# Routed expert layer in two halves of tiles, with the neighbouring stages' work between its slots

## What is computed

```python
x = x + tanh(g_xattn[2]) * L2_xattn(layernorm(x), ctx, ctx, ...)      # L2: 16 heads, one shared key/value head
x = x + tanh(g_ffn[2])   * L2_ffn(layernorm(x), switch_w, ..., w1, b1, w2, b2)   # F2: the routed experts
x = x + tanh(g_xattn[3]) * L3_xattn(layernorm(x), ctx, mask, ...)     # L3: causal, with masked queries
x = x + tanh(g_ffn[3])   * L3_ffn(layernorm(x), ...)                  # F3: butterfly weights

# L2_ffn: of 8 experts each token uses the one with the largest probability
logits = t @ switch_w + switch_b
route_prob = softmax(logits)
y_e = gelu(t @ w1[e] + b1[e]) @ w2[e] + b2[e]
out = y_(argmax e) * max(route_prob)
```

## Time and profile before

| | us |
|---|---|
| runs, median (lowest to highest) | 1117.06 (1116.2 to 1119.53) |
| profiled execution, first to last instruction | 1124.8 |
| TensorE / VectorE / ScalarE / POOL busy | 932.1 / 754.2 / 677.1 / 454.1 |
| end of L2's statistics to L3's first scores | 691.5 to 844.3 |

### The profile page before, as it was taken

One profiled execution on the slowest core, in us unless ns is written; L12 is line 12 of the kernel. 1 busy time (PEld: TensorE's weight loads), 2 busy tenths in 40 slices (PEclk: granted clock), 3 DMA queues, 4 the chain that ended last, 5 costly groups with the idle time before them and its releaser, 6 DMA issues.

```text
span 1124.8 us, 29016 instructions
## 1 busy us (share of the span) xinstructions
PE 932.1 (83%) x9406; PEld 555.3 (49%) x9416; DVE 754.2 (67%) x2004; ACT 677.1 (60%) x1462; POOL 454.1 (40%) x975
## 2 busy tenths in 40 slices
PE   3898889885758565799999886599958999999899
PEld 3644444443436333344545443277733555454698
DVE  3566777756978799778887772355584666667444
ACT  3556666646856566767776641155535777775466
POOL 5411112241134434301244344344458988877300
PEclk9999999995559777899999995599989999999999
DMA  6977656429999300000000000112131111111011
GB/s 186 155 88 82 47 45 47 38 29 238 179 181 174 97 1 1 1 1 2 2 15 15 14 11 19 39 51 60 54 84 58 40 58 40 59 55 43 6 36 35
DMA packets 285283, 67.07 MB, mean 60 GB/s; under 512 B 206241, under 2 KB 277985, under 8 KB 285154
## 3 DMA queue, kind: packets, MB, share of 16 engines
q1 hardware_dynamic: 279394, 50.94, 29.6%
q0 software_dynamic: 4896, 14.18, 3.7%
q10 hardware_dynamic: 864, 0.27, 0.1%
HBM read 34.80 MB, written 30.56 MB: 58 GB/s over the span
## 4 chain that ended last, share of the span: by engine, by line
PE 57%; DVE 21%; issue 8%; POOL 6%; ACT 3%; DMA 2%; SPq 2%; another core or an unknown queue 1%; DVEq 0%; ACTq 0%; POOLq 0%
PE bank L1132 14%; DVE nmax L1580 8%; PE bank L1164 6%; PE bank L1446 3%; PE bank L1431 3%; PE bank L1248 3%; PE bank L1146 3%; PE bank L1486 3%; PE bank L1478 2%; DVE stats L1515 2%; DVE small L1760 2%; PE bank L1257 2%; PE bank L1135 2%; PE bank L1122 2%; PE bank L1439 2%
## 5 line engine op out<-in xcount | busy, mean ns | idle before, releaser
L1580 DVE TENSOR_REDUCE nmax<-bank 128x8 f32<-128x1024 f32 x192 | 234.8, 1223 | 129.1 <-PE bank L1135 126.4
L823 ACT ACTIVATE probs_space<-bank 128x1024 f32<-128x1024 f32 x192 | 196.7, 1024 | 153.5 <-PE bank L1146 152.6
L1132 PE MATMUL bank<-q_one,k_all 32*128 32x512 f32 x768 | 221.5, 646 | 30.3 <-DVE nmax L1580 27.4
L1135 PE MATMUL bank<-k_one,q_all 32*128 32x512 f32 x768 | 218.4, 643 | 2.4 <-DVE nmax L1580 1.1
L1164 PEld LDWEIGHTS bank<-probs_space,vals 128*32 128x32 f32 x3072 | 74.3, 110 | 125.7 <-issue 124.1
L1164 PE MATMUL bank<-probs_space,vals 128*32 128x128 f32 x3072 | 127.8, 284 | 0.0
L1132 PEld LDWEIGHTS bank<-q_one,k_all 32*128 32x128 f32 x768 | 62.6, 187 | 59.9 <-issue 57.9
L833 ACT ACTIVATE k_one<-k_all,one_head 128x512 f32<-128x512 f32 x96 | 68.8, 722 | 20.8 <-DVE k_all L1606 19.3
L1146 PE MATMUL bank<-nmax_one,ones_bf 12*128 12x512 bf16 x384 | 79.3, 385 | 0.0
L576 POOL TENSOR_TENSOR var_b<-stats 128x8 f32<-128x8 f32 (+3 forms) x32 | 7.2, 225 | 178.4 <-DVE stats L1515 176.2
L649 POOL CAST nmax_parts<-nmax 128x16 bf16<-128x16 f32 x64 | 12.7, 199 | 162.9 <-DVE nmax L1580 121.4
(11 more groups left out here) (282 smaller groups left out, 2248.7 us busy)
## 6 DMA issues: line engine op xcount, KB each, us to landing
expert_rows<-zeros SPq DMA_DIRECT2D x8, 2128.5 KB, 31.8
late<-in_L_ffn_up_weights_dram POOLq DMA_DIRECT2D x9, 512.0 KB, 4.1
late<-_L_ffn_down_weights_dram POOLq DMA_DIRECT2D x9, 512.0 KB, 4.2
q_one<-expert_rows SPq DMA_DIRECT2D x40, 64.5 KB
q_scratch<-late SPq DMA_DIRECT2D x8, 256.0 KB
v_scratch<-moe_w SPq DMA_DIRECT2D x8, 256.0 KB, 3.4
vals<-v_scratch SPq DMA_DIRECT2D x8, 256.0 KB, 6.9
o_scratch<-o_tok SPq DMA_DIRECT2D x32, 64.0 KB, 3.1
```

Source lines behind the costliest of these rows:

```text
L823: act.activation(probs[:, 2 * g:2 * g + 2, :, :].rearrange("k g i q -> k (g i q)"), bank_pair[1][:, :, :].rearrange("k g f -> k (g f)"), A ...
L1132: pe.matmul(bank[2 + s], group(k_all, u, 2 * g + s), group(q_one, u, 2 * g + s), start=not masked, stop=False)
L1135: m = pe.matmul(bank[s], group(q_all, v, 2 * f + s), group(k_one, v, 2 * f + s), start=not masked, stop=True)
L1580: dve.tensor_reduce(nmax[:, u % 2, 0, :].rearrange("q (g i) -> q g i", i=HG)[:, 2 * g:2 * g + 2, :], bank_pair[0][:, :, :].rearrange("q g ...
```

## The change

- **Two halves.** PARTS = 2: tiles 0 to 15 and 16 to 31 have their own regions in expert_rows, their own slot table and 23 slots each, NS = 46. starts_0 and ends hold the row sums per half.
- **Routing between slots.** L2 is run up to iteration 33; iterations 34 to 40 stand before slot steps -2, 5, 6, 7, 8, 9 and 11 (ROUTE_BEFORE) on TensorE, ScalarE and VectorE. POOL does the rows and scatters of the last two quads after its slots 3, 5, 7 and 9. The slots start on the first half's table alone. VectorE makes the second table in four blocks at steps 12 to 15.
- **Expert weights stationary.** VectorE copies the slot's expert's w1 (128x512) within SBUF to hid2, with a register load of its own (of_next); TensorE multiplies its four 128-column parts, stationary, with the transposed slot, so the result is already transposed. The four transposes (L1439) and the copy out of PSUM (L1883) go, the seven fill products too. VectorE now has two register loads per slot.
- **Masks** of L3 in six blocks at steps 16 to 21; keep_rep lies in three other buffers. W_con is loaded before L1 rather than at the end of L2, and transposed at step 13.
- **Return.** The first half's rows are loaded by SP before slot 31 and added by VectorE two tiles at a time at steps 30 to 37; POOL makes norms of the first 16 tiles after its slots 31, 33 and 37. The second half's rows are added inside L3, at its iterations 2 to 8; their norms are made by POOL at its tiles 7 and 12.
- **Head of L3.** Iterations -10 to -7 run before step 36, -6 to -3 before steps 40 to 43 (LAST_HEAD), on TensorE and ScalarE; the fill products of the head go.
- **POOL's schedule in L3**: three butterfly steps a tile only up to step 18, then four; none at tiles 7, 12 and 18, which have a norm.

```diff
...
+        ROUTE_BEFORE = {-2: NT + 2, 5: NT + 3, 6: NT + 4, 7: NT + 5, 8: NT + 6, 9: NT + 7, 11: NT + 8}
+        SECOND_TABLE_FROM, TRANSPOSED_AT, MASKS_FROM = 12, 13, 16
+        RETURN_FROM = 30
+        LAST_HEAD = {NS - 10: range(-X_LEAD, -6), NS - 6: (-6,), NS - 5: (-5,), NS - 4: (-4,), NS - 3: (-3,)}
...
@@ SP
                 for s_no in range(NS):
+                    if s_no % NS_PART == 0:
+                        part = s_no // NS_PART
+                        sp.wait_ge(S("R_slots"), part + 1)
+                        for c in range(4):
+                            sp.wait_ge(S(f"scattered_{c}"), 16 * QT * (part + 1))
+                    if s_no == NS_PART + RING:
+                        returned_rows(0)
...
@@ POOL, beside_last_attention
-                pool.wait_ge(S("B_res"), NT)
+                pool.wait_ge(S("R_gate"), PARTS)
...
-                    if v == 16:
+                    if v == 7:
+                        norms(6 * NT, 16, 24, keep_scale=True)
+                    elif v == 12:
+                        norms(6 * NT, 24, NT, keep_scale=True)
+                    elif v == 18:
                         norms(7 * NT, 0, 8)
-                    for _ in range(3 if k < 6 * STAGES else 4):
+                    for _ in range(0 if v in (7, 12, 18) else 3 if k < 2 * STAGES else 4):
...
@@ POOL, after the indirect DMA of slot s_no
+                    if s_no == 3:
+                        rows_of_quad(NQ - 2)
+                    elif s_no == 5:
+                        scatter(NQ - 2)
+                    elif s_no == 7:
+                        rows_of_quad(NQ - 1)
+                    elif s_no == 9:
+                        scatter(NQ - 1)
+                    elif s_no == 11:
+                        pool.wait_ge(S("t_pv"), 2 * 2 * NT)
+                        pool.iota(column_no, [[-HR, HG], [1, P]], base=0, channel_multiplier=0,
...
@@ ScalarE
-                for t in range(-2, iterations("L2").stop):
+                for t in range(-2, NT + 2):
...
                 for t in range(-2, NS):
+                    if t in ROUTE_BEFORE:
+                        iteration(ROUTE_BEFORE[t])
+                    for i in LAST_HEAD.get(t, ()):
+                        last_iteration(i)
...
+                routing_weights(1)
...
@@ TensorE
-                load_expert(0)
-                fill_wait(7)
+                pe.wait_ge(S("t_mx"), 2 * 2 * NT)
+                pe.wait_ge(S("t_ex"), 2 * 2 * NT)
                 for t in range(-2, NS + 1):
...
+                    if t == TRANSPOSED_AT:
+                        last_weights()
...
                     if live(t + 1, NS):
                         pe.wait_ge(S("G_xe"), t + 2)
-                        past(pe, "G_hs", t)
-                        pe.matmul(bank[(t + 1) % 2][:, :], xnT[:, (t + 1) % 2, :],
-                                  moe_w1[:, bass.ds(expert[t + 1] * HID, HID)], start=True, stop=True
-                                  ).then_inc(S("G_hp"), 1)
...
+                        past(pe, "G_ge", t)
+                        pe.wait_ge(S("G_w1"), t + 2)
                         for c in range(NC):
...
+                            m = pe.matmul(bank[(t + 1) % 2][:, c * P:(c + 1) * P],
+                                          hid2[:, (t + 1) % 2, c * P:(c + 1) * P], slot_xT[:, (t + 1) % 2, :],
+                                          start=True, stop=True)
+                        m.then_inc(S("G_hp"), 1)
+                    load_expert(t)
...
@@ VectorE
+                for t in range(-2, NS + 1):
+                    if t in ROUTE_BEFORE:
+                        iteration(ROUTE_BEFORE[t])
+                    if live(t + 2, NS):
+                        if t + 2 == NS_PART:
+                            dve.wait_ge(S("R_slots"), 2)
+                        of_next = dve.value_load(expert_int[0:1, t + 2:t + 3], min_val=0, max_val=NE - 1)
+                        past(dve, "G_hp", t + 1)
+                        dve.tensor_copy(hid2[:, t % 2, :], moe_w1[:, bass.ds(of_next * HID, HID)]).then_inc(S("G_w1"), 1)
                     if live(t + 1, NS):
-                        dve.wait_ge(S("G_hp"), t + 2)
-                        past(dve, "G_ht", t)
-                        dve.tensor_copy(hid[:, (t + 1) % 2, :], bank[(t + 1) % 2][:, :]).then_inc(S("G_hs"), 1)
+                        dve.wait_ge(S("G_xt"), t + 2)
...
+                    if 0 <= t - SECOND_TABLE_FROM < 4:
+                        slot_table(1, t - SECOND_TABLE_FROM)
+                    if 0 <= t - MASKS_FROM < 6:
+                        last_masks(t - MASKS_FROM)
+                    if 0 <= t - RETURN_FROM < NT_PART // 2:
+                        add_returned(2 * (t - RETURN_FROM), 2 * (t - RETURN_FROM) + 2)
...
+                iteration = attention("L3")
+                for t in range(-2, iterations("L3").stop):
+                    if t == -2:
+                        gates_of(1)
+                    if 2 <= t < 5:
+                        add_returned(NT_PART + 3 * (t - 2), NT_PART + min(3 * (t - 1), GC))
+                    if 5 <= t < 9:
+                        add_returned(NT_PART + GC + 2 * (t - 5), NT_PART + GC + 2 * (t - 4))
+                    iteration(t)
```

More of the change, by code:

```diff
@@ L817, in quad_bank @@
                 def quad_bank(c):
-                    return bank[2] if own and c == 0 else bank[5]
+                    return bank[2] if layer == "L2" and c == 0 else bank[5]
                 def exponentials(u, g):
@@ L911, in attention @@
                 return iteration
-            def run(layer):
-                iteration = attention(layer)
-                for t in iterations(layer):
-                    iteration(t)
             def bit_ffn(layer, gated, steps, next_iteration=None):
@@ L1392, in _ @@
             if "L2" in phases:
[L1393 removed]
+                for t in range(-2, NT + 2):
                     iteration(t)
             if "F2" in phases:
[L1396 to L1401 removed]
+                last_iteration = attention("L3")
                 pe.wait_ge(S("t_ve"), NQ)
@@ L1450, in _ @@
             if "L3" in phases:
-                run("L3")
+                for t in range(-2, iterations("L3").stop):
+                    last_iteration(t)
             if "F3" in phases:
@@ L1592, in by_group, with iteration @@
                     return ap.rearrange("q (g i) -> q g i", i=HG)
-                for t in iterations(layer):
-                    if between is not None and t > NT:
-                        between(t - 1)
+                def iteration(t):
                     u, v, w = t - lag, t + 2, t - R_XT
@@ L1694, in attention @@
                             dve.sem_inc(S("wsum"), 1)
+                return iteration
             def mask_rows():
@@ L1800, in first_steps @@
                     bit_ffn("F0", False, range(t - NT - 4, t - NT - 3))
-            attention("L0", first_steps)
+            iteration = attention("L0")
+            for t in iterations("L0"):
+                if t > NT:
+                    first_steps(t - 1)
+                iteration(t)
             if "F0" in phases:
@@ L1839, in _ @@
             if "L2" in phases:
-                attention("L2")
+                iteration = attention("L2")
+                for t in range(iterations("L2").start, NT + 2):
+                    iteration(t)
             if "F2" in phases:
-                dve.wait_ge(S("R_start"), NQ)
-                link(dve.tensor_scalar(fill[:, 0, :], starts[:, QT, :], 1.0 / P, (P - 1) / P - 0.498, ALU.mult, ALU.add))
-                link(dve.tensor_scalar(fill[:, 0, :], fill[:, 0, :], MAGIC, None, ALU.add))
@@ new lines, in add_returned @@
+                def add_returned(first, last):
+                    part = first // NT_PART
+                    for t in range(first, last):
+                        at = (t - part * NT_PART) * P
+                        if t % GC == 0:
+                            dve.wait_ge(S(f"chunk_in{t // GC}"), 32)
+                        dve.scalar_tensor_tensor(out=x[:, t * P:(t + 1) * P], in0=returned[part][:, at:at + P],
+                                                 scalar=gate[:, t:t + 1], in1=x[:, t * P:(t + 1) * P],
+                                                 op0=ALU.mult, op1=ALU.add).then_inc(S("B_res"), 1)
+                    dve.wait_ge(S("B_res"), last)
+                    for t in range(first, last):
+                        tile_stats(t)
@@ new lines, in _ @@
+                for step in range(4):
+                    slot_table(0, step)
+                gates_of(0)
+                dve.wait_ge(S("w_exp"), 32)
+                dve.wait_ge(S("t_s2"), 2 * 2 * NT)
+                for t in range(-2, NS + 1):
+                    if t in ROUTE_BEFORE:
+                        iteration(ROUTE_BEFORE[t])
+                    if live(t + 2, NS):
[4 more added lines that the diff above has]
+                        dve.tensor_copy(hid2[:, t % 2, :], moe_w1[:, bass.ds(of_next * HID, HID)]).then_inc(S("G_w1"), 1)
```

(10 more changed lines are left out.)

309 lines of the change are left out of this document (174 added, 135 removed).

## The result

The changed kernel took 1127.57 us, the median of four runs (1124.01 to 1134.86), against 1117.86 for the kernel before (1116.2 to 1119.53): a ratio of 1.0093, 95% interval 1.0048 to 1.0138. Slower by 0.9%, where 1125 was forecast. The total came out as forecast, but two of its terms did not, and they cancelled.

A forecast was written before the change was run, and what follows sets the result against it. VectorE's queue, register loads included, was to bound the slots and POOL most of early L3. +2 us up to L3 and +5.5 in L3, total +7.7 on 1117.06, gave 1125 us; own range 1112 to 1138, all cases 1100 to 1142.

The forecast's parts named there:

- To the first slot's add: From L2's last statistics at 691.5 to 709.1: table 4.3, gates 0.9, routed iteration 3.0, first load and copy 1.2, start-up 8.2.
- The slot: Steady slot: VectorE's queue round of 2.16 us exceeds TensorE's 1.90, so VectorE becomes the bound; range 2.05 to 2.43.
- The F3 loop does exactly this mix per tile: TensorE's slot work: priced by an F3 tile of the same transposes and products, 1.90 us where it needed 2.30.
- rival 1: Slots: TensorE stays the bound at 1.90 us, register loads hidden; L3 starts 26 us earlier, total 1097; chance 0.25.
- What stands between the slots: Work put between slots counts in full on VectorE: routing 7.7, table 5.1, masks 8.7, returns 9.3, head 9.0 us.
- head of L3: L3's first iterations placed between slots 36 and 43: 9 us, floor 3, ceiling 10.4, its time alone.
- start-up of 8.2: Slot stretch: 8.2 us counted on top of the full slot steps, taken over unchanged from the kernel before.
- The schedule's part: L3: POOL's denser butterfly steps and added norms, 12.4 us more work up to tile 19, partly absorbed, leave about +5.
- VectorE's 16 adds and statistics (7.7 us) at tiles 2 to 8 lie mostly where POOL binds: +0.5: L3: adding the second half's returned rows there is mostly hidden behind POOL and costs only 0.5 us.
- rival 3: Slots with blocks in them: TensorE's low busy share drops the clock, +12 us over 24 slots, total 1137; chance 0.11.
- rival 4: Slots: each weight copy waits for POOL's indirect DMA, 0.74 us in each of 46, +34, total 1159; chance 0.06.
- rival 2: L3 takes no harm: POOL's split, a tile ahead, absorbs the dense stretch; +2 only, total 1119; chance 0.14.

The follow-up runs named there:

- e6: The kernel before with only the stationary expert weights added (40 slots, no halves), one register load per slot on VectorE: 1111.47 us, ratio 0.9959.
- e4: The changed kernel with one register load of the expert's number per slot on VectorE, kept for the output add: 1116.01 us, ratio 1.0014.
- e1: The changed kernel without the 16 adds of the second half's returned rows in L3 (output incomplete): 1115.76 us, ratio 1.0014.
- e9: The changed kernel with only POOL's step count altered: three per tile to step 54, then five, none at tiles 7, 12, 18: 1122.06 us, ratio 1.0067.
- e7: The changed kernel with one register load per slot, four wide adds, and POOL at three steps per tile to step 54, then five: 1099.35 us, ratio 0.9851.
- e2: The changed kernel with the second half's returned rows scaled by ScalarE and added in four wide instructions instead of sixteen: 1118.60 us, ratio 1.0031.
- e5: The kernel before with only the stationary expert weights added (40 slots, no halves), two register loads per slot on VectorE: 1110.21 us, ratio 0.9954.
- e10: The changed kernel itself, unchanged, timed and profiled a second time: 1124.47 us, ratio 1.0086 against the kernel before.
- e3: The changed kernel with POOL's butterfly steps as in the kernel before, three per tile to step 54, then four: 1122.42 us, ratio 1.0070.

## Why the prediction was right, and where it was not

The forecast was slower, 1125 us, in a range of 1100 to 1142, and 1127.57 was measured. By its own steps:

- *To the first slot's add*, forecast 17.6 us from the last statistics: 17.1. The table alone, forecast 4.3: 4.2, 680.74 to 684.93.
- *The slot*, forecast 2.16, VectorE's round of 0.80, 0.35 and 1.01: 2.13, of 0.77, 0.34 and 1.02. Right, and the copy at 0.42 was 0.43. But **the step "The F3 loop does exactly this mix per tile", and so "TensorE needs 1.90", failed**. Of the F3 loop's tile the products are the same, yet a slot takes 2.10 with a register load less (e6) and 2.16 in e4. Of the 0.3 us of idle TensorE time per slot next to nothing was there (busy 10.52 of the 10.62 us of the five steady slots from 763.05). VectorE set the slot by 0.03 us at most, and rival 1, 1097 us from a slot of 1.90, did not come. What makes the 0.2 was not tried; a slot has a register load, addresses worked out from it and a wait for ScalarE's activations that the F3 loop has not.
- *What stands between the slots*, each sum of intervals less 2.13 a slot: routing forecast 7.7, measured 5.8; second table 5.1 and 5.1; masks 8.7 and 9.2; returned rows 9.3 and 7.2; head of L3 9.0, measured 5.0 (3.4 with the last slots' speeding up in it, which the forecast has in its start-up of 8.2: that counts 39 full steps, and in the kernel before the last ones were shorter). **The head was the term furthest off**: I took 9 between a floor of 3 and a ceiling of 10.4, by the row that was nearest, and the slots' work and the head's overlapped far better than that. Forecast for the whole stretch +2.2, measured -7.7: 9.9 too high, of which 4.0 are the head, 2.1 the start with the last slots' speeding up, 2.1 the returned rows, 1.9 the routing and 1.4 the slots at 2.13 for 2.16; the masks and a few longer slots stand against them.
- *L3*, forecast +5.5, measured +15.9. The schedule's part, forecast +5, was right: L3 kept 6.1 without the adds (e1), and mending the schedule gave back 4.7 with the sixteen adds in place (e9) and 6.9 with the four wide ones (e7 against e2). **The step that failed is "VectorE's 16 adds and statistics (7.7 us) at tiles 2 to 8 lie mostly where POOL binds: +0.5"**. The adds cost 9.8. I had priced them by the earlier trace rows, where POOL ran nothing wide, and had looked for a collision only where the change adds an instruction, not where it moves one.
- *The clock* (rival 3) did not fall for the slots: between the first slot's add and the last it was lower from 755.6 to 762.4 only, beside the widest mask products. It did fall in L3, for 13.6 us in three stretches, each behind or inside a stall of TensorE.
- *The copy and POOL's transfer* (rival 4) hardly hindered each other: of the 46 copies 33 ran beside a transfer, and 29 of these took 0.43. The other four took 0.50 to 0.75, 0.6 us too long in all, where 34 were priced. *L3 takes no harm* (rival 2) is out by 15.9 us.

Two errors of about 10 us with opposite signs made the sum right, and that was luck. So was the direction: without the adds, which were priced at 0.5, the kernel is not slower at all (e1, 1.0014, 0.9983 to 1.0045). What did hold is the reason given for the stretch ahead of L3, that six more slots and 40 us of work on VectorE eat up what the overlap gives: with the stationary weights in both, the halves brought 1.4 us there (e5 and e10, 147.9 and 146.5).

**The rule that did hold.** I weighed one sentence of the Trainium skill, page "SBUF — State Buffer", section "Who interferes with whom", that on copies in a two-port mode, against the rows and found it not to hold; here 29 of 33 copies beside a transfer say so again, and the four that were longer say that it is not out altogether. The same section has a second sentence that I passed over: a VectorE instruction with two inputs in SBUF contends with a GpSimd instruction that reads SBUF, and the one that comes second waits for the whole of the first. By that, the moved adds (returned rows and x, both in SBUF) had to wait beside the butterfly products. The trace agrees: 0.34 against a median of 1.02 us. Instructions of VectorE with only one input in SBUF were spared. In L3 the residual add of the attention (L1729), whose other input is in PSUM, took 0.34 to 0.35 in all its 32 instances, 11 of them beside such a product (full or half size), and the statistics, with one input, 0.27 to 0.30, 34 of 48 beside one.

## What to carry to other kernels

A step that is moved keeps its count of instructions, not its price: look up what the other engines run at the new place, and for VectorE whether its instruction has two operands in SBUF while POOL streams wide ones. If it must stand there, make it few and long (four waits in place of sixteen), or see whether one operand can be in PSUM; for these adds that was not tried. And before work is put between the steps of a loop, find the engine that bounds the loop and take from it what it does twice: the register load that was made two times per slot decided whether the overlap of the halves was worth 1.4 us or 10 to 12.

## What the runs showed of the hardware

- VectorE and POOL exclude each other by the instruction, in both directions, when VectorE reads two operands in SBUF: the add 0.34 to 1.66, POOL's cast 0.20 to 0.75. Beside POOL's short operations on 4 to 16 columns the add stayed at 0.33 to 0.35; so it did in the kernel before at 831, beside a power of POOL of 1.05 us on 4 columns.
- POOL's indirect transfer stayed at 0.96 to 1.13 beside copies, adds and small operations, and 42 of the 46 copies took 0.43 to 0.44, beside it or not. Of the four others two, of 0.50, began 0.04 us ahead of a transfer, one of 0.55 in the last third of one, and that of 0.75 at the end of one and beside a 512-wide operation of POOL. What did stretch the transfer are the mask products, with two operands in SBUF: to 2.23 us twice by those of 1536 columns and to 1.70 by that of 1024.

```profile
748.41 0.97 POOL L808 DMA_INDIRECT token_rows<-q_one,slot_row_int  x1 [2.41 <-DVE q_one L2025]
751.75 2.23 POOL L808 DMA_INDIRECT token_rows<-q_one,slot_row_int  x1 [2.37 <-DVE q_one L2025]
...
751.39 1.75 DVE L1981 TENSOR_TENSOR quant_bf<-ident_blocks,keep_all 128x1536 bf16<-128x1536 f32 x1
```

- The granted clock differs for the same work. After L3's last tile TensorE was busy 5.17 of 7 us in e5 and 5.16 of 7 in the kernel before; in e5 the clock was at its lower level for most of the ten us that followed, which cost 3.6 us of what the slots had gained, and in the kernel before it was not. In all twelve kernels here TensorE was busy 5.16 or 5.17 us of those seven (12.6 to 19.6 us after the last tile's maxima); after them the clock was lower for 10.3 us in e5 and e6, for 3.4 in e3, e4 and e9, where the stretch after L3 was 1.6 us longer, and not at all in the other seven. What decides it is open.

```profile
1034.00:1041.00 7.00, 5.17 (x60) 2.98 (x61) 2.25 (x9) 2.24 (x6) 0.00 (x0) 1.00 0.01 2
1041.00:1051.00 10.00, 9.58 (x40) 7.81 (x39) 4.02 (x12) 3.42 (x10) 3.93 (x10) 0.52 0.00 0
```
```profile
1050.00:1057.00 7.00, 5.16 (x58) 2.86 (x54) 2.50 (x9) 1.99 (x5) 0.00 (x0) 1.00 0.00 0
1057.00:1067.00 10.00, 8.98 (x72) 7.99 (x71) 5.38 (x18) 5.66 (x18) 3.95 (x10) 1.00 0.03 8
```

The first pair is e5, the second the kernel before; the granted clock is the third number from the end.
